# Turning half of a layer's inputs on VectorE instead of TensorE, and reordering two handovers between layers

## What is computed

```python
x = _layernorm(x + _L0_gnn_ref(x, adj, ...), axis=-1)   # layer 1: attention from h h^T, three weights, twice
x = _layernorm(x + _L1_gnn_ref(x, adj, ...), axis=-1)   # layer 2, twice:
    m_left, m_right, h_lin = h @ W_left[l].T, h @ W_right[l].T, h @ W_lin[l].T + b_lin[l]
    u = u_left * adj_tri + u_left * diag_mask + u_right * swapaxes(adj_tri)   # u_left = h m_left^T / sqrt(384)
    a = exp(u) * adj;  a = a / (sum(a) + 1e-10)
    h = relu(layer_norm(a @ h_lin))
x = _layernorm(x + _L2_gnn_ref(x, ...), axis=-1)        # layer 3: 12 heads
x = _layernorm(x + _L3_gnn_ref(x, adj, ...), axis=-1)   # layer 4: 12 heads, masked
```

## Time and profile before

| | us |
|---|---|
| median of 3 runs | 2672.84 |
| lowest and highest run | 2670.54, 2675.16 |
| the profiled execution's own time | 2675.72 |
| its span (first to last instruction) | 2673.9 |
| TensorE busy | 2597.9 |
| VectorE busy | 1963.5 |
| ScalarE busy | 1245.8 |
| GpSimd busy | 1521.1 |

### The profile page before, as it was taken

How to read it: one execution, slowest core, us unless ns; L and a number is a source line. 1 busy time by engine, 2 the same in 40 slices (tenths; PEclk the granted TensorE clock), 3 DMA queues, 4 the chain that set the end, 5 groups by cost and what they waited for, 6 DMA issues and landing times.

```text
span 2673.9 us, 59544 instructions
## 1 busy us (share of the span) xinstructions
PE 2597.9 (97%) x23232; PEld 2261.9 (85%) x23232; DVE 1963.5 (73%) x4469; ACT 1245.8 (47%) x2433; POOL 1521.1 (57%) x1380
## 2 busy tenths in 40 slices
PE   8999999999997999999999997999999999999997
PEld 7998999999986888888888876888888888888886
DVE  5788888888876556555655657888888877777775
ACT  2344444344343344444444443554555555556554
POOL 7657756756756666666666654544344344555553
PEclk9999999999998999999999998999999999999998
DMA  5012111111115012111111123123332212423422
GB/s 161 32 42 69 55 54 58 58 51 58 51 50 153 24 49 60 35 41 54 43 37 51 36 73 89 51 64 76 76 76 76 76 52 75 102 76 88 101 76 74
DMA packets 219496, 175.43 MB, mean 66 GB/s; under 512 B 141776, under 2 KB 217168, under 8 KB 219216
## 3 DMA queue, kind: packets, MB, share of 16 engines
q1 hardware_dynamic: 219216, 171.62, 23.0%
HBM read 121.25 MB, written 50.33 MB: 64 GB/s over the span
## 4 chain that ended last, share of the span: by engine, by line
PE 90%; DVE 3%; POOL 2%; issue 2%; ACT 1%; DMA 0%; POOLq 0%; ACTq 0%; SPq 0%; DVEq 0%
PE bank L1362 15%; PE bank L316 14%; PE bank L815 11%; PE bank L1370 11%; PE pair L815 11%; PE bank L1422 4%; PE pair L1391 4%; PE bank L1408 3%; PE bank L300 3%; PE pair L300 3%; PE bank L801 2%; PE bank L329 2%; PE bank L839 2%; PE pair L839 2%; PE bank L286 1%
## 5 line engine op out<-in xcount | busy, mean ns | idle before, releaser
L1802 POOL TENSOR_TENSOR h_logits<-h_logits,h_mx 128x512 f32<-128x512 f32 x192 | 202.7, 1056 | 284.7 <-DVE h_mx L1645 284.7
L1657 DVE TENSOR_TENSOR h_val<-bank,h_rowvec 64x192 f32<-64x192 f32 x512 | 181.6, 355 | 35.1 <-PE bank L1370 26.0
L382 ACT ACTIVATE l_sides<-bank 128x512 f32<-128x512 f32 x192 | 114.3, 596 | 192.9 <-PE bank L316 192.8
L1099 POOL TENSOR_TENSOR l_hlo<-l_hf,l_hhi 128x576 fp32r<-128x576 f32 x96 | 134.7, 1432 | 115.1 <-ACT l_hhi L932 115.1
L1362 PE MATMUL bank<-h_hhia,whi 128*128 128x512 f32 x432 | 179.2, 415 | 7.9 <-POOL h_hlob L1809 7.6
L1522 ACT ACTIVATE h_keys<-bank,h_keycol,h_halves 128x512 f32<-128x512 f32 x192 | 139.0, 776 | 82.2 <-PE bank L1362 82.2
L1008 DVE TENSOR_TENSOR l_val<-bank,l_vec 64x384 f32<-64x384 f32 x256 | 142.3, 556 | 40.8 <-PE bank L815 37.8
L1362 PE MATMUL bank<-h_hhia,wlo 128*128 128x512 f32 x432 | 170.9, 396 | 0.0
L1008 DVE TENSOR_TENSOR l_val<-pair,l_vec 64x384 f32<-64x384 f32 x256 | 142.3, 556 | 35.9 <-PE pair L815 32.1
L1138 POOL TENSOR_TENSOR l_vdiag<-l_vdiag,l_vec 128x384 f32<-128x384 f32 x128 | 127.7, 1018 | 66.2 <-ACT l_vdiag L913 66.1
L453 DVE TENSOR_TENSOR l_val<-bank,l_vec 128x384 f32<-128x384 f32 x64 | 35.6, 556 | 152.6 <-PE bank L300 152.6
(11 more groups left out here) (259 smaller groups left out, 7829.2 us busy)
## 6 DMA issues: line engine op xcount, KB each, us to landing
h_strips<-x SPq DMA_DIRECT2D x128, 192.0 KB, 5.1
l_hf<-xt SPq DMA_DIRECT2D x16, 864.0 KB, 5.2
l_x<-x SPq DMA_DIRECT2D x16, 768.0 KB, 4.5
l_x<-x SPq DMA_DIRECT2D x32, 384.0 KB, 3.2
...
```

The costliest lines, as they stand in the source:

```text
L1099: nc.gpsimd.tensor_tensor(hlo[:, c, :], hf[:, c, :], hhi[:, c, :], ALU.subtract).then_inc(lo_done, 1)
L1657: ins = nc.vector.tensor_tensor(val[S * p:S * p + S, 2 * t + b, :, p, 0:HD], src[rows, :, p, :], bias[rows, :, p, :], ALU.add)
L1802: nc.gpsimd.tensor_tensor(row, row, mx[:, c, :, ts].unsqueeze(3).broadcast_to([P, HP, 2, S]), ALU.subtract).then_inc(sub_done, 1)
```

## The change

**Layer 2, inputs from x.** For the 16 slots with `from_x`, TensorE's 12 matmuls and ScalarE's three copies go. In their place SP loads the group as four strips (`load_strips`) into a tile `blocks` that lies over `hf`. In slot n it does so for slot n + 2, behind the adjacency of that slot and behind `u_done` and `lo_done`. VectorE turns the tile in place (`rows_turned`) and casts from it (`high_parts`), both at the start of slot n for slot n + 1, ahead of `final_sum` and `values_out`; the cast stood behind `final_shift` before. GpSimd's `low_parts` and TensorE's `pair_scores` read `blocks`. x as rows is still loaded, for `final_sum`. The host permutes the first sublayer's weights.

**Handover from layer 1 to 2.** `strips(0)` is issued in layer 1's last slots but one, `strips(1)` ahead of x(0). On VectorE `rows_turned(0)` stands ahead of layer 1's last `diagonal`, and `rows_turned(1)` with `high_parts(1)` ahead of the first `split_weights`. TensorE no longer transposes there.

**Handover from layer 2 to 3.** VectorE does `one_side(31)`, `deltas(31)` and the values first, and layer 3's `rows_turned(0)` and `low_parts(0)` behind them; ScalarE does the exponential first, then `high_parts(0)`, `context_out(31)`, and only then `final_apply(14)`, which is what the store of group 14 waits for. `rows_turned(1)` goes from slot 0 of layer 3 into the preamble, ahead of `final_sum(15)`, whose two halves now have two `maxima` and a `values_out` between them. `high_parts(1)` goes ahead of a wait on ScalarE, `low_parts(1)` on GpSimd ahead of the last three of six `take_off`.

```diff
+    blocks = [nc.alloc_sbuf_tensor_at(f"l1_blocks{a}", [P, BLOCKS, KC, SQ], F32, offset=at)
+              for a, at in zip("ab", (sh.rows_at, sh.at_hfb))]
...
+        def load_strips(n):
+            for j in range(STRIPS):
+                sync.dma_start(blocks[n % 2][SQ * j:SQ * j + SQ, :, :, :].rearrange("p b c a -> p b (c a)"),
+                               strips_in[group(n)][:, :, RUN * j:RUN * j + RUN]).then_inc(strips_loaded[n % 2], 16)
+
         first = rows.first
+        sync.wait_ge(first.stored[0], 16)
+        load_strips(0)
+        yield
+        sync.wait_ge(first.u_done, first.passes)
+        sync.wait_ge(first.lo_done, KC * first.passes)
+        sync.wait_ge(first.stored[1], 16)
+        load_strips(1)
...
+                if from_x(n + 2):
+                    sync.wait_ge(u_done, n + 1)
+                    sync.wait_ge(lo_done, KC * (n + 1))
+                    load_strips(n + 2)
...
+                elif n and from_x(n):
+                    pe.wait_ge(ml_evac, 2 * KC * (n - 1) + (5, 6, 3)[k])
...
+                            keys = blocks[n % 2][:, 2 * g + half, c, :] if from_x(n) else \
+                                hf[n % 2][:, c, g * S + Q * half:g * S + Q * half + Q]
...
-                transposes(n + 1)
+                if not from_x(n + 1):
+                    transposes(n + 1)
...
             if n + 1 < 4 * iters:
-                chunks(n + 1)
-            else:
-                next(after)
-            for g in finished(n):
-                final_apply(g)
+                if not from_x(n + 1):
+                    chunks(n + 1)
+                for g in finished(n):
+                    final_apply(g)
             act.wait_ge(mx_done, n + 1)
             nc.scalar.activation(e[:, :, :].rearrange("p t (h i) -> p t h i", h=2), ut[:, :, :, 0, :], ACT.Exp, scale=scale).then_inc(e_done, 1)
+            if n + 1 == 4 * iters:
+                next(after)
             context_out(n)
+        for g in finished(4 * iters - 1):
+            final_apply(g)
...
+        def rows_turned(n):
+            dve.wait_ge(strips_loaded[n % 2], 16 * STRIPS * (n // 4 + 1))
+            nc.vector.transpose(blocks[n % 2][:, :, :, :], blocks[n % 2][:, :, :, :]).then_inc(xt_done, 1)
+
         def high_parts(n):
             for c in range(KC):
-                dve.wait_ge(f_done, KC * n + c + 1)
                 dve.wait_ge(v_done, max(NPROJ * (n - 1), 0))
-                nc.vector.tensor_copy(hhi[n % 2][:, c, :], hf[n % 2][:, c, :]).then_inc(hi_done, 1)
+                if from_x(n):
+                    dve.wait_ge(xt_done, entered(n))
+                    nc.vector.tensor_copy(hhi[n % 2][:, c, :].rearrange("p (b r) -> p b r", r=SQ),
+                                          blocks[n % 2][:, :, c, :]).then_inc(hi_done, 1)
+                else:
+                    dve.wait_ge(f_done, KC * turned(n) + c + 1)
+                    nc.vector.tensor_copy(hhi[n % 2][:, c, :], hf[n % 2][:, c, :]).then_inc(hi_done, 1)
...
+            dve.wait_ge(x_loaded[g % XBUFS], 32 * (g // XBUFS) + 16 * (half + 1))
...
+            if n + 1 < 4 * iters and from_x(n + 1):
+                rows_turned(n + 1)
+                high_parts(n + 1)
             split_weights(sh, dve, "hi", *weights_of_slot(i, s))
...
             if n + 1 < 4 * iters:
-                high_parts(n + 1)
-            else:
-                next(after)
+                if not from_x(n + 1):
+                    high_parts(n + 1)
...
         final_sum(4 * iters - 1, groups - 1, 0)
+        next(after)
         final_sum(4 * iters - 1, groups - 1, 1)
         final_stats(groups - 1)
...
+                if from_x(n):
+                    upper, lower = (part[n % 2][:, c, :].rearrange("p (b r) -> p b r", r=SQ) for part in (hhi, hlo))
+                    nc.gpsimd.tensor_tensor(lower, blocks[n % 2][:, :, c, :], upper, ALU.subtract).then_inc(lo_done, 1)
+                else:
+                    nc.gpsimd.tensor_tensor(hlo[n % 2][:, c, :], hf[n % 2][:, c, :], hhi[n % 2][:, c, :],
+                                            ALU.subtract).then_inc(lo_done, 1)
...
+            if n + 2 == passes:
+                next(after)
...
+            if n + 1 == passes:
+                next(after)
             diagonal(n)
             deltas(n)
...
+        rows_turned(1)
         yield
         additive_mask(0)
         maxima(0, 0)
-        yield
         maxima(0, 1)
         dve.wait_ge(vec_in, 16 * 3)
         values_out(0, 0)
+        yield
...
-                rows_turned(1)
                 maxima(0, 3)
...
-        for k in range(2 * (KC - 1)):
+        for k in range(3):
             take_off(0, k)
+        low_parts(1)
+        take_off(0, 3)
...
-            if n == 0:
-                low_parts(1)
...
+        if name.startswith("L1_gnn_W"):
+            turn = v[0][strip_order()]
+            v = np.stack([turn if name.endswith("lin") else turn[:, strip_order()], v[1]])
```

49 lines of the change are left out of this document (24 added, 25 removed).

## The result

The changed kernel took 2657.0 us in the median of four runs (2652.6 to 2657.5), beside 2674.0 for the kernel before: a ratio of 0.9931, with a 95% interval of 0.9918 to 0.9943. A second measurement on another occasion gave 2654.5 beside 2676.9, 0.9919 (0.9905 to 0.9932). The forecast was 2656.7.

The account below looks back on a forecast made before the run. TensorE, busy for 97% of the span, was taken as the bound. Steady slots -9.1, first handover -3.4 and second handover -3.6 summed to -16.1 us, from the median 2672.8 to 2656.7 us; range 2644 to 2674.

Parts of the forecast that it names:

- TensorE's saving: Layer 2's steady slots: each of 14 groups of transposes taken off TensorE frees 1.40 us, 19.6 us offered.
- What steady slots give back: Layer 2: of 2.8 us per pair, 1.2 (s = 0) and 0.3 (s = 3) are lost; seven pairs give -9.1 us.
- Loss in s = 0: Layer 2's slots with s = 0: 6.8 us of added VectorE stretch against 6.5 of room; 1.2 us lost, bounds 0 and 3.5.
- First handover: Layer 1 to 2: context(0) starts at 833.8 instead of 837.27, -3.4 us, bounds -6 and -1.
- Context(31): Layer 2 to 3: its 3.97 us wait for VectorE goes, as layer 3's work moves behind `deltas`; -4.0 us.
- Behind context(31): Second handover: later strips lengthen waits on scores and values, but `query_key(1)` loses its 7.6 us wait, starting 3.6 us earlier.
- a sign of being wrong: Second handover: a wait on scores of over 8 us would show the forecast wrong.
- Full cover: Rival for the steady slots: strips land before `normalise` ends and casts run nearly free; 2644 us, chance 0.15.
- eaten: Rival: steady slots lose 2.8 us per pair and the second handover gives nothing; -3.4, 2669 us, chance 0.20.
- slower: Rival: VectorE late in every slot with s = 0, +2.2 us per pair; 2684.8 us, chance 0.12.
- The other sign of being wrong: Layer 2's steady slots: a wait of over 2 us for strips in each pair would show the forecast wrong.
- The worst row for casts: Upper bound for three casts in a steady slot: 5.9 us, taken beside GpSimd's 1152-column work; forecast 3.7.

Follow-up runs that it names:

- the power first: The changed kernel with GpSimd's final_power ahead of the masks in slots with s = 0; 2651.1 us, ratio 0.9897 to the kernel before.
- the kernel with the strips ahead: The changed kernel with layer 2's strips for slot n + 2 issued ahead of the adjacency's loads; 2653.5 us, ratio 0.9908 to the kernel before.
- the kernel with the handover alone: The kernel before with only the second handover's edits and the buffer choice; 2666.6 us, ratio 0.9967 to the kernel before.
- The experiment with the strips first: The changed kernel with layer 3's second strips issued ahead of group 14's store and the twelve loads; 2641.8 us, ratio 0.9866 to the kernel before.
- the kernel with the buffer choice back: The changed kernel with the choice of high parts' buffer in layers 3 and 4 and its two waits as before; 2659.4 us.

## Why the prediction was right, and where it wasn't

- **TensorE's saving.** Forecast 1.40 us a slot; a clean slot is 1.31 shorter (23.91 to 22.60). 14 of them offer 18.3, not 19.6. The term was read from the start of the next instruction in one slot; whole slot periods would have been the better row.
- **What steady slots give back.** Forecast 1.3 a pair, -9.1 for seven. Measured from context(3) to context(31), less the wait of context(31): 668.5 us before, 659.3 after, -9.2. That stretch holds only six of the seven slots with s = 3; slot 3 was 1.3 shorter too where its clock was full (23.84 to 22.53 with the power first), so a pair gives 1.5 and seven 10.5. The parts in slot 16: wait for strips 1.8 (said 1.3), transposition 1.78 (1.77), casts 2.84 (3.7), the stretch 6.5 (6.8); in the other slots the casts take 2.75 to 3.56 and the stretch 6.0 to 7.6. Loss in s = 0 0.93 to 1.25 (1.2); in s = 3 nothing (0.3).
- **The reason given for that loss was half wrong.** The working let it come from the spread of the strips' wait and longer z steps. The longer z steps are real: the power starts 17.9 us behind context(15), where it was 17.3. The strips' wait has next to no part in it, 0.3 us each in two slots, as the kernel with the strips ahead shows. GpSimd's queue sets it: z steps, masks, then the power, and then the low parts, which hold `final_shift` for 1.1 us. The change itself made that last item: `hi` is now ready early, so `low_parts` follows the power at once, where it waited 0.6 us for its casts before. The forecast took the low parts for granted and never asked what their earlier start would meet.
- **First handover.** Forecast -3.4, context(0) at 833.8; measured -3.5, at 833.76. That close it is luck: in the eleven traces with this handover context(0) starts at 832.8 to 836.0, 834.7 in the mean, 2.6 less than the 837.3 and 837.4 of the two without it. Slot 1 behind it is shorter as well, 27.5 us in all eleven against 29.3 and 28.4, and that stands in no term.
- **Context(31).** Forecast -4.0; measured 3.97 of wait gone, the same in the kernel with the handover alone.
- **Behind context(31).** Forecast +0.4 at the first `query_key` of group 1, with strips landing at 1612 (11.6 of VectorE's idle time was their price). At that mark it is +1.9, so 2.1 us are gained there and not 3.6; part of the difference is the new wait of 2.3 us for layer 3's first low part, which no term has. At the sixth scores it is +0.6 and +1.3 in two traces and +0.1 in the kernel with the handover alone. The path was as told: the wait of 7.6 us goes, and the second scores wait 10.1 instead of 2.45. The prediction had named a wait on scores of over 8 us here as a sign of being wrong. The sign is there, and it did not fit the prediction's own terms: with the `maxima` 3.6 later and TensorE 4 sooner, a wait of 2.45 becomes 10. The experiment with the strips first shows that this was no law: 11 us lay there.
- **The missed term.** The new choice of buffer with its shifted waits was in the change and in no step of the sum; no line of the working speaks of it. It gives 4.5 us at the start of layer 4, in every trace. By the forecast's own terms and this one the sum would have been -20.6, 2652 us, where the two measurements gave -17.0 and -22.4. The forecast's median was so met a little by luck; either is inside the range. The fair test of the terms that were priced is the kernel with the buffer choice back: 17.5 us under the kernel before, beside the forecast 16.1. The row that would have shown it stood in the list of waits: the `query_key` line had three waits of 10.0 us, of which the prediction used only the longest, 7.6.
- **The rivals.** Full cover did not come with this change, and it needs two small edits elsewhere; "eaten" and "slower" asked for losses of 2.8 and 5 us a pair, against 1.1 measured (slots with s = 0 are 23.60 to 23.92 us long, a clean one 22.60). The other sign of being wrong, over 2 us of waiting for strips in each pair, was also there (3.5 us on average), and cost next to nothing, since GpSimd was later still. The worst row for casts (5.9 us beside 1152 columns) was no guide for casts beside work of 384 columns, as was said against it.
